# Decoder layer: value projection moved ahead of queries and keys, its place among the first scores taken by context rows

## The chip, the cores and the metric

The kernel runs on one core of one Trainium2 chip. The metric is the device time of one execution in microseconds. Three executions of the kernel before took 847.68, 848.48 and 849.51 us; the median is 848.48 us.

## The reference

One post-norm decoder layer on x (2 sequences of 256 tokens, width 512, fp32) with a context of 2 x 512 rows:

```python
# 1. causal self-attention, 32 heads of 16, ALiBi bias
qkv = x @ w_attn + b_attn                       # w_attn 512 x 1536: q, k, v
scores = einsum('bqhd,bkhd->bhqk', q, k) / 16
attn = softmax(where(causal, scores + slope[h] * (k_pos - q_pos), -inf))
x = layernorm(x + (attn @ v) @ w_proj + b_proj)
# 2. cross-attention: 32 query heads, 8 key/value heads of 128
kv = concat([context, x], axis=1)               # 768 rows per sequence
q = rms_norm(x @ Wq) * q_norm_w;  k = rms_norm(kv @ Wk) * k_norm_w;  v = kv @ Wv
x = layernorm(x + softmax(q k^T / sqrt(128)) @ v @ Wo)
# 3. feed-forward by blocks of a permuted x, 16 blocks of 32 -> 128 -> 32
x = layernorm(x + ffn(x))
```

## The kernel before, in words

All large products are made in three passes of 512 columns on TensorE (`three_passes`, lines 46 to 50): each fp32 operand is split into a high and a low part, and hi x hi, hi x lo and lo x hi are summed in one PSUM bank. So every weight chunk (128 x 512, one of four of a 512 x 512 group) goes through a fixed chain: SP's DMA queue loads it into `w_raw[:, i, :]`, ACT makes `w_hi` (`weights_hi`, line 474), and DVE (`early_lo`, line 617) or POOL (`late_lo`, line 408) makes `w_lo = raw - hi`. There is one raw buffer of four chunks, so the load of chunk i of group p waits until `w_lo` of chunk i of group p - 1 is made (`load_weights`, line 336).

The first stage (the function that the diff touches) computes the self-attention, and at the same time keys and values of the cross-attention for all 12 row tiles of context and x1. Its parts:

- 16 transposes of x (line 802) and their split into `xT_hi` (ACT, line 524) and `xT_lo` (DVE, line 675).
- Q and K, 48 matmuls each: bank 4 + m for the m-th tile of 128 features. ACT takes Q out (`qT`, line 535). K is taken out twice, for even heads by ACT (`kT_even`, line 543) and for odd heads by DVE (`kT_odd`, line 690).
- V, 48 matmuls, by row tile j (`values(j)`, line 821); ACT takes each tile out in two pieces (line 552).
- 16 quads of four heads each. For quad c: scores "S" (line 844, banks 0 to 3, 16 matmuls that stream past 32 rows each); "E" for each of its four heads: DVE adds the bias and takes the maximum (`softmax_shift`, line 628), ACT exponentiates (line 485); "R": DVE makes reciprocals (line 637), POOL multiplies by them (lines 421 and 423) and makes the biases of the next quad (`alibi`, line 416); "T": transposes (line 854), copied out by DVE (line 643); "PV": the product with the values for a pair of quads.
- "part" (n, r): an eighth of the keys and values of context or x1 row tile n, six matmuls. Four column groups (two of Wk, two of Wv) take two parts each. "CT"/"CX" transpose and split a context tile, "KG" copies keys out and squares them on ACT (lines 515 and 520), DVE sums the squares (line 666), POOL normalises (lines 449 and 451), "KT"/"KX" transpose the keys.

The order is written out by one function, `order_of_work`, as a list that every engine walks through, doing only its own share of each entry. Each engine works strictly in that order. S(c + 1) waits until DVE has done all four heads of quad c (`s_out`), since the banks are the same. Bank order beside that is planned in a loop over the list (`RING` banks 4 and 7, `GROUPS` banks 5 and 6).

Weight groups are loaded in the order p = 0, 1, 2 (q, k, v of `w_attn`), 3, 4 (`Wk`), 5, 6 (`Wv`), 7 (`w_proj`), 8, 9 (`Wq`). `ON_VECTOR` lists the groups whose low part is DVE's work; those in `ON_POOL` are POOL's. "W" p in the list is the place where a later group is split. The entry "XT" 1 / "XL" 1 at quads 11 and 12 writes x1's second row tile over the scores' banks; the next scores wait for its low part (DVE, line 721).

Before, the list begins S0, W5, V0, E(0,0), V1, E(0,1), V2, E(0,2), CT0, CX0, V3, E(0,3), R(0,0), W6, R(0,1), and then S1 with part(0,0), E(1,0), T(0,0) and so on.

Of the kernel before, what the change touches and what calls it, by code (L numbers as in the profile page):

```python
# [23 lines left out]
KT = D // P  # L24
# [57 lines left out]
def order_of_work():  # L82

    order = [("S", 0), ("W", 5), ("V", 0), ("E", (0, 0)), ("V", 1), ("E", (0, 1)), ("V", 2), ("E", (0, 2)), ("CT", 0), ("CX", 0), ("V", 3),
             ("E", (0, 3)), ("R", (0, 0)), ("W", 6), ("R", (0, 1))]
# [27 lines left out]

    for c in range(NQ):
# [5 lines left out]
        for i in range(QUAD):  # L120
            late = []
            if mid == 0 and i == 2:
                parts(q % 2)
                copy_keys(q // PARTS, q % PARTS // 2 - 1)
# [6 lines left out]
            elif mid == 1 and i < 3:  # L131
                if i == 1:
                    copy_keys(q // PARTS, q % PARTS // 2 - 1)
# [27 lines left out]
        if c < NQ - 1:  # L161
            parts(1)
# [50 lines left out]
def self_attention_and_keys(nc, d, k):  # L213

    with ExitStack() as ctx:
# [7 lines left out]
        ON_VECTOR, ON_POOL = (0, 1, 2, 4, 6, 8), (3, 5, 7)  # L223
# [60 lines left out]
        before = {4: ("V", 0), 7: ("V", 3), 5: ("V", 1), 6: ("V", 2)}  # L284
# [49 lines left out]
        def _(sp):  # L334
            def load_weights(p):
                name, g = (("w_attn", 0), ("w_attn", 1), ("w_attn", 2), ("Wk", 0), ("Wk", 1), ("Wv", 0), ("Wv", 1),
                           ("w_proj", 0), ("Wq", 0), ("Wq", 1))[p]
                for i in range(KT):
                    if p > 0 and p - 1 in ON_VECTOR:
                        sp.wait_ge(w_los, KT * ON_VECTOR.index(p - 1) + i + 1)  # L340
                    elif p > 0:
                        sp.wait_ge(late_los, KT * ON_POOL.index(p - 1) + i + 1)
# [7 lines left out]
            for i in range(TT):  # L350
                sp.dma_start(x[:, i, :], d["x"].rearrange("b s d -> (b s) d")[tokens(i), :]).then_inc(x_in[i], 16)
# [37 lines left out]
        def _(pool):  # L389
# [38 lines left out]
            late_lo(3)  # L428
            late_lo(5)
# [41 lines left out]
        def _(act):  # L471
# [49 lines left out]

            for j in range(TT):
# [3 lines left out]
            for i in range(KT):  # L526
                weights_hi(0, i)
            act.wait_ge(col_ps, 1)
            nc.scalar.activation(cols[:], bank[:, 7, 0:NCOLS], ACT.Copy).then_inc(col_out, 1)
            for i in range(KT):  # L530
                weights_hi(1, i)
            act.wait_ge(col_out, 1)
# [5 lines left out]
            for i in range(KT):  # L538
                weights_hi(3, i)
            act.wait_ge(nw_made, 2)  # L540
            for m in range(KT):
# [3 lines left out]
                weights_hi(4, m)  # L545
            act.wait_ge(zeros, 2)
            for what, a in ORDER:
                if what == "V":
                    act.wait_ge(v_ps, a + 1)
                    for odds in range(2):  # L550
                        lanes = slice(odds * SA_DIM, (odds + 1) * SA_DIM)
# [1425 lines left out]
```

## Time and profile before

| | before |
|---|---|
| median of three runs | 848.48 us |
| profiled execution, its own time | 847.78 us |
| span of its trace | 846.0 us |
| mean granted TensorE clock | 0.996 |
| PE busy | 825.7 us, 98% of the span |
| DVE, POOL, ACT busy | 547.8, 522.1, 475.4 us |

The span lies 1.8 us below the execution's own time, and the profiled execution is 0.7 us below the median. Times of the trace count from the start of the span. "PE" is the matmul queue, "PEld" its weight loads, "SPq" the issue of DMAs by SP. A timeline row gives start, length, engine, line of the kernel, instruction, output and inputs, and in square brackets the engine's idle time before it with what ended it. The matmuls overlap: a 128x512 matmul is shown with some 0.4 us, but the next begins 0.23 to 0.24 us after it began.

### The profile page before, as it was taken

What the parts mean: (1) busy time and instruction counts of PE and PEld (TensorE: products, weight loads), DVE (VectorE), ACT (ScalarE), POOL (GpSimd) and SP (SyncE); (2) the same over time, 40 slices, a digit from 0 to 9 for tenths busy, and PEclk for the clock granted to TensorE, in tenths of its full rate; (3) what the DMA queues carried; (4) which work ended last, traced back from release to release, by engine and by line L of the source; (5) the groups of instructions that cost most, each with busy time, mean ns of one, the idle gap of its engine ahead of it and who ended that gap; (6) DMA issues with size and microseconds to landing.
All of it is one profiled execution on the core that took longest, in us unless ns stands there. A gap on an engine that the chain in (4) does not pass through costs nothing. (4 is left out here: it accounts for less than half of the span.)

```text
span 846.0 us, 15109 instructions
## 1 busy us (share of the span) xinstructions
PE 825.7 (98%) x4841; PEld 693.0 (82%) x4841; DVE 547.8 (65%) x1505; ACT 475.4 (56%) x1005; POOL 522.1 (62%) x676
## 2 busy tenths in 40 slices
PE   7999999999999999999999999999999999999986
PEld 5777777777788888888888888888888888888764
DVE  4466566765345776667666766677667767777654
ACT  5666665566246565555555555556455645556543
POOL 3577876767336566765766666765775676536741
PEclk9999999999999999999999999999999999999999
DMA  7613223121141721221102101122122102000011
GB/s 226 186 38 117 84 75 109 55 76 51 50 138 54 250 77 38 69 69 39 50 24 86 62 21 68 37 68 68 37 68 68 37 4 76 4 0 1 1 26 50
DMA packets 48510, 56.22 MB, mean 66 GB/s; under 512 B 4670, under 2 KB 29772, under 8 KB 48460
## 3 DMA queue, kind: packets, MB, share of 16 engines
q1 hardware_dynamic: 48460, 55.59, 21.5%
q8 instruction: 27, 0.44, 0.2%
q14 instruction: 23, 0.19, 0.1%
HBM read 41.95 MB, written 13.63 MB: 66 GB/s over the span
## 5 line engine op out<-in xcount | busy, mean ns | idle before, releaser
L1251 POOL TENSOR_SCALAR prob<-prob,x_rinv 128x768 f32<-128x768 f32 x124 | 112.6, 908 | 173.4 <-DVE x_rinv L1425 173.4
L1362 ACT ACTIVATE pT_hi<-bank 128x512 fp32r<-128x512 f32 x192 | 114.3, 598 | 90.1 <-PE bank L1575 90.0
L1345 ACT ACTIVATE prob<-bank,x_nm,q_rms 128x768 f32<-128x768 f32 x124 | 123.3, 995 | 47.2 <-DVE x_nm L1419 46.7
L1465 DVE TENSOR_TENSOR pT_lo<-bank,pT_hi 128x512 fp32r<-128x512 f32 x192 | 130.2, 679 | 5.1 <-ACT pT_hi L1362 3.7
L1416 DVE TENSOR_REDUCE x_mx<-bank 128x1 f32<-128x768 f32 x124 | 118.3, 954 | 22.0 <-PE bank L1529 21.6
L1575 PE MATMUL bank<-ident,prob 128*128 128x128 f32 x768 | 114.8, 272 | 2.1 <-POOL prob L1251 1.3
L1575 PEld LDWEIGHTS bank<-ident,prob 128*128 128x128 f32 x768 | 95.0, 140 | 14.0 <-POOL prob L1251 2.0
L48 PE MATMUL bank<-pT_hi,xv_hi 128*128 128x512 f32 x192 | 86.5, 450 | 1.2 <-DVE pT_lo L1465 0.8
L485 ACT ACTIVATE s_self<-s_self,nm_self 128x128 f32<-128x128 f32 (+1 forms) x128 | 57.1, 448 | 43.1 <-DVE nm_self L628 42.6
L50 PE MATMUL bank<-pT_hi,xv_lo 128*128 128x512 f32 x192 | 75.7, 394 | 0.0
L49 PE MATMUL bank<-pT_lo,xv_hi 128*128 128x512 f32 x192 | 75.4, 393 | 0.0
L1529 PE MATMUL bank<-xk_hi,qT_hi 128*128 128x384 f32 x244 | 65.6, 350 | 0.3 <-ACT prob L1345 0.2
L1529 PE MATMUL bank<-xk_lo,qT_hi 128*128 128x384 f32 x244 | 63.4, 341 | 0.0
L1529 PE MATMUL bank<-xk_hi,qT_lo 128*128 128x384 f32 x244 | 62.7, 337 | 0.0
L48 PE MATMUL bank<-wq_hi,x_hi 128*128 128x512 f32 x144 | 58.8, 408 | 0.0
L1371 ACT ACTIVATE oT_hi<-bank 128x512 fp32r<-128x512 f32 x32 | 19.2, 599 | 69.5 <-PE bank L50 69.5
L50 PE MATMUL bank<-wq_hi,x_lo 128*128 128x512 f32 x144 | 56.6, 393 | 0.0
L49 PE MATMUL bank<-wq_lo,x_hi 128*128 128x512 f32 x144 | 56.4, 392 | 0.0
L48 PE MATMUL bank<-w_hi,cT_hi 128*128 128x512 f32 x128 | 56.0, 437 | 0.0
L643 DVE COPY pT_self<-bank 128x384 f32<-128x384 f32 x64 | 35.4, 554 | 29.3 <-PE bank L854 29.1
L48 PE MATMUL bank<-wo_hi,oT_hi 128*128 128x512 f32 x128 | 52.3, 409 | 0.0
L1529 PEld LDWEIGHTS bank<-xk_hi,qT_hi 128*128 128x128 f32 x244 | 43.5, 189 | 9.5 <-ACT prob L1345 1.5
(227 smaller groups left out, 2043.1 us busy)
## 6 DMA issues: line engine op xcount, KB each, us to landing
wo_raw<-in_Wo SPq DMA_DIRECT2D x8, 1024.0 KB, 5.4
v_by_head<-v_st SPq DMA_DIRECT2D x12, 512.0 KB, 3.3
kT_by_head<-kT_st SPq DMA_DIRECT2D x12, 512.0 KB, 3.2
xk_raw<-kT_by_head SPq DMA_DIRECT2D x16, 384.0 KB, 3.2
xv_raw<-v_by_head SPq DMA_DIRECT2D x16, 384.0 KB, 3.2
wq_raw<-in_Wq SPq DMA_DIRECT2D x6, 1024.0 KB, 5.5
wq_raw<-in_w_attn SPq DMA_DIRECT2D x12, 256.0 KB, 3.9
xk_raw<-in_ctx SPq DMA_DIRECT2D x8, 256.0 KB, 2.6
```

Of the source, the lines that this page charges most:

```text
L48: nc.tensor.matmul(out, a_hi, b_hi, start=first, stop=False)
L49: nc.tensor.matmul(out, a_hi, b_lo, start=False, stop=False)
L50: return nc.tensor.matmul(out, a_lo, b_hi, start=False, stop=last)
L485: nc.scalar.activation(s_sb[:, c % 2, i, a:e], s_sb[:, c % 2, i, a:e], ACT.Exp, bias=nm[:, c % 2, i, qt:qt + 1], scale=-1.0, accum_out=rsu ...
L643: nc.vector.tensor_copy(pT[:, c % 2, i, :], bank[:, bank_of("T", (c, i)), 0:3 * P]).then_inc(pt_out, 1)
L1251: nc.gpsimd.tensor_scalar(prob[:, s, :], prob[:, s, :], rinv[:, s:s + 1], 1.0, ALU.mult, ALU.mult)\
L1345: nc.scalar.activation(prob[:, s, :].rearrange("p (a e) -> p a e", a=2), bank[:, at:at + 2, 0:HALF], ACT.Exp, bias=nm[:, s:s + 1], scale=q ...
L1362: nc.scalar.activation(pT_hi[:, a, :], bank[:, turn.bank[s, what, a], :], ACT.Copy)\
L1416: nc.vector.reduce_max(mx[:, s:s + 1], bank[:, at:at + 2, 0:HALF], AX.XY)\
L1465: nc.vector.tensor_tensor(pT_lo[:, a, :], bank[:, turn.bank[s, what, a], :], f32(pT_hi[:, a, :]), ALU.subtract).then_inc(ring_out, 1)
L1529: last = nc.tensor.matmul(bank[:, at + c, 0:HALF], a_hi[:, g, w], k_part[:, b, c * HALF:(c + 1) * HALF], start=start, stop=stop)
L1575: last = nc.tensor.transpose(bank[:, at, j * P:(j + 1) * P], prob[:, UT * (s % 2) + j, a * P:(a + 1) * P], ident[:])
```

## The change

- The weight groups of `w_attn` are loaded in the order v, q, k. The loads of x and of the v group alternate on SP's queue (x tile 0, chunk 0, x tile 1, chunk 1, ...).
- V is made first, in 16 steps of three matmuls (chunk i, row tile j), as tiles and chunks arrive; the transposes of x tiles 2 and 3 stand among them. ACT and DVE split x tiles and v chunks in turn. Then come the transpose of the bias columns (now into bank 0), Q and K.
- The "V" entries leave the list. CT0 and CX0 go ahead of S0, and two parts stand where two V tiles were. The list begins CT0, CX0, S0, W6, part(0,0), E(0,0), part(0,1), E(0,1), R(0,0), KG(0,0), part(0,2), E(0,2), part(0,3), E(0,3), R(0,1), then S1, KG(0,1), part(0,4).
- Four parts come sooner in that way, and four part entries that stood at the end of quads leave (`if c < NQ - 5`): those ahead of S13, S14, S15, and the one behind T(14,3) in quad 14.
- `w_lo` of groups 3 and 5 moves from POOL to DVE. The split of group 5 moves from the list to the loop that takes K out; groups 3 and 4 are both split between Q's last and K's first eviction.
- The four additions of the projection bias on POOL are no longer behind eight `w_lo`.

Core of the diff:

```diff
-    order = [("S", 0), ("W", 5), ("V", 0), ("E", (0, 0)), ("V", 1), ("E", (0, 1)), ("V", 2), ("E", (0, 2)), ("CT", 0), ("CX", 0), ("V", 3),
-             ("E", (0, 3)), ("R", (0, 0)), ("W", 6), ("R", (0, 1))]
+    order = [("CT", 0), ("CX", 0), ("S", 0), ("W", 6)]
...
+    for i in range(QUAD):
+        parts(1)
+        order.append(("E", (0, i)))
+        if i % 2:
+            order.append(("R", (0, i // 2)))
...
-        if c < NQ - 1:
+        if c < NQ - 5:
             parts(1)
...
-        ON_VECTOR, ON_POOL = (0, 1, 2, 4, 6, 8), (3, 5, 7)
+        ON_VECTOR, ON_POOL = (0, 1, 2, 3, 4, 5, 6, 8), (7,)
...
# SP
-                name, g = (("w_attn", 0), ("w_attn", 1), ("w_attn", 2), ("Wk", 0), ("Wk", 1), ("Wv", 0), ("Wv", 1),
+                name, g = (("w_attn", 2), ("w_attn", 0), ("w_attn", 1), ("Wk", 0), ("Wk", 1), ("Wv", 0), ("Wv", 1),
                            ("w_proj", 0), ("Wq", 0), ("Wq", 1))[p]
                 for i in range(KT):
+                    if p == 0:
+                        sp.dma_start(x[:, i, :], ...)
...
# ACT
             for m in range(KT):
+                weights_hi(2, m)
                 act.wait_ge(qk_ps, m + 1)
                 nc.scalar.activation(qT[:, m, :], bank[:, 4 + m, :], ACT.Identity, bias=cols[:, m:m + 1])\
                     .then_inc(q_out, 1)
-                weights_hi(2, m)
-            for i in range(KT):
-                weights_hi(3, i)
+            for p in (3, 4):
+                for i in range(KT):
+                    weights_hi(p, i)
             act.wait_ge(nw_made, 2)
             for m in range(KT):
                 act.wait_ge(qk_ps, KT + m + 1)
                 nc.scalar.activation(kT_even[:, m, :], ...)
-                weights_hi(4, m)
+                weights_hi(5, m)
...
# PE
+            def values(i, j):
+
+                pe.wait_ge(xt_lo, j + 1)
+                pe.wait_ge(w_los, i + 1)
+                last = three_passes(nc, bank[:, 4 + j, :], xT_hi[:, i, tokens(j)], xT_lo[:, i, tokens(j)],
+                                    w_hi[:, 0, i, :], w_lo[:, 0, i, :], i == 0, i == KT - 1)
...
+            row_transposes(0)
+            row_transposes(1)
+            values(0, 0)
+            row_transposes(2)
+            for i, j in ((0, 1), (1, 0), (1, 1)):
+                values(i, j)
+            row_transposes(3)
+            for i, j in ((0, 2), (1, 2), (2, 0), (2, 1), (2, 2), (0, 3), (1, 3), (2, 3)):
+                values(i, j)
+            for j in range(TT):
+                values(KT - 1, j)
```

DVE before, from the last of K's odd heads to the first shifts of quad 0 (`kT_odd` is K for odd heads, `w_lo` a weight chunk's low part, `s_self` the shifted scores):

```order
L690 TENSOR_SCALAR kT_odd<-bank,cols,odd 128x512
L617 TENSOR_TENSOR w_lo<-wq_raw,w_hi 128x512
L628 ISA s_self,nm_self<-bank,alibi 128x128
L628 ISA nm_self 128x1
L628 ISA s_self,nm_self<-bank,alibi 128x256
```

The same place of the changed kernel (here its line numbers are two or three higher):

```order
L693 TENSOR_SCALAR kT_odd<-bank,cols,odd 128x512
L619 TENSOR_TENSOR w_lo<-wq_raw,w_hi 128x512
L623 TENSOR_TENSOR cT_lo<-bank,cT_hi 128x512
L619 TENSOR_TENSOR w_lo<-wq_raw,w_hi 128x512 x4
L630 ISA s_self,nm_self<-bank,alibi 128x128
L630 ISA nm_self 128x1
L630 ISA s_self,nm_self<-bank,alibi 128x256
```

The low part of context tile 0 and the four low parts of group 6 now stand ahead of the first shift.

PE before, from the transposes T(11,3) (line 854) over part(6,7) to the scores S13 (line 844):

```order
L854 MATMUL bank<-ident,s_self 128x128 x3
L48 MATMUL bank<-w_hi,cT_hi 128x512
L49 MATMUL bank<-w_lo,cT_hi 128x512
L50 MATMUL bank<-w_hi,cT_lo 128x512
L48 MATMUL bank<-w_hi,cT_hi 128x512
L49 MATMUL bank<-w_lo,cT_hi 128x512
L50 MATMUL bank<-w_hi,cT_lo 128x512
L844 MATMUL bank<-kT_odd,qT 128x128 x4
L844 MATMUL bank<-kT_odd,qT 128x256 x4
```

The same place of the changed kernel, from part(7,2) over T(11,3) (now line 870) to S13 (now line 860):

```order
L48 MATMUL bank<-w_hi,cT_hi 128x512
L49 MATMUL bank<-w_lo,cT_hi 128x512
L50 MATMUL bank<-w_hi,cT_lo 128x512
L48 MATMUL bank<-w_hi,cT_hi 128x512
L49 MATMUL bank<-w_lo,cT_hi 128x512
L50 MATMUL bank<-w_hi,cT_lo 128x512
L870 MATMUL bank<-ident,s_self 128x128 x3
L860 MATMUL bank<-kT_odd,qT 128x128 x4
L860 MATMUL bank<-kT_odd,qT 128x256 x4
```

The six matmuls between T(11,3) and S13 have left; part(6,7) now stands in front of T(11,0), at the start of quad 12's scores.

## Rows read from the trace of the kernel before

**Rows 1.** The page: engine totals and the granted clock over 40 slices.
```profile
span 846.0 us, 15109 instructions
...
PE 825.7 (98%) x4841; PEld 693.0 (82%) x4841; DVE 547.8 (65%) x1505; ACT 475.4 (56%) x1005; POOL 522.1 (62%) x676
...
PEclk9999999999999999999999999999999999999999
```

**Rows 2.** Windows: busy time by engine in each stretch, last columns clock and DMA.
```profile
3.36:7.05 3.69, 3.69 (x16) 3.08 (x16) 1.39 (x3) 1.79 (x3) 3.44 (x5) 1.00 1.03 339
7.05:9.15 2.10, 0.00 (x0) 0.03 (x1) 2.10 (x4) 2.06 (x5) 0.45 (x2) 1.00 0.44 165
9.15:10.17 1.02, 1.01 (x4) 0.84 (x5) 1.02 (x3) 0.61 (x2) 0.00 (x0) 0.99 0.23 14
10.17:13.67 3.50, 3.50 (x9) 2.34 (x7) 0.64 (x2) 0.00 (x0) 0.00 (x0) 0.52 0.80 252
13.67:33.70 20.03, 20.03 (x86) 15.88 (x85) 9.62 (x16) 13.17 (x23) 5.08 (x4) 1.00 0.70 213
33.70:57.00 23.30, 22.55 (x131) 17.16 (x134) 12.10 (x48) 16.13 (x50) 16.23 (x21) 1.00 0.26 84
57.00:220.00 163.00, 162.51 (x1192) 126.52 (x1192) 101.90 (x385) 102.11 (x313) 115.40 (x220) 1.00 0.27 81
```

**Rows 3.** Timeline of PE: start, length, instruction, idle before it.
```profile
9.15 0.47 PE L48 MATMUL bank<-x_hi,w_hi 128*128 128x512 f32 x1 [2.10 <-DVE w_lo L617]
...
33.70 0.94 PE L844 MATMUL bank<-kT_even,qT 32*128 32x128 f32 x16
...
46.62 0.94 PE L844 MATMUL bank<-kT_odd,qT 32*128 32x128 f32 x16
...
56.86 0.94 PE L844 MATMUL bank<-kT_even,qT 32*128 32x128 f32 x16 [0.53 <-DVE nm_self L628]
...
176.65 0.94 PE L844 MATMUL bank<-kT_odd,qT 32*128 32x128 f32 x16
```

**Rows 4.** Timeline of ACT, first 40 us.
```profile
4.48 0.60 ACT L524 ACTIVATE x_hi<-bank 128x512 fp32r<-128x512 f32 x1 [2.46 <-PE bank L802]
...
22.57 0.69 ACT L535 ACTIVATE qT<-bank,cols 128x512 f32<-128x512 f32 x1 [1.51 <-PE bank L50]
...
27.53 0.63 ACT L474 ACTIVATE w_hi<-wq_raw 128x512 fp32r<-128x512 f32 x1 [2.05 <-DMA wq_raw<-in_Wk]
28.07 0.76 ACT L543 ACTIVATE kT_even<-bank,even_bias,even 128x512 f32<-128x512 f32 x1
...
33.81 0.78 ACT L543 ACTIVATE kT_even<-bank,even_bias,even 128x512 f32<-128x512 f32 x1 [1.51 <-PE bank L50]
...
39.12 0.63 ACT L474 ACTIVATE w_hi<-wq_raw 128x512 fp32r<-128x512 f32 x1 [2.21 <-DMA wq_raw<-in_Wv]
```

**Rows 5.** Timeline of DVE at 5, 35 and 175 us.
```profile
5.12 0.69 DVE L675 TENSOR_TENSOR x_lo<-bank,x_hi 128x512 fp32r<-128x512 f32 x1 [3.55 <-ACT x_hi L524]
...
35.42 0.68 DVE L617 TENSOR_TENSOR w_lo<-wq_raw,w_hi 128x512 fp32r<-128x512 f32 x1
36.02 0.28 DVE L628 CUSTOM_DVE_ANT_0 s_self<-bank,alibi 128x128 f32<-128x128 f32 x1
...
36.58 0.28 DVE L628 CUSTOM_DVE_ANT_0 s_self<-bank,alibi 128x128 f32<-128x128 f32 x1
...
175.35 0.55 DVE L643 COPY pT_self<-bank 128x384 f32<-128x384 f32 x1
175.82 0.68 DVE L721 TENSOR_TENSOR x_lo<-bank,x_hi 128x512 fp32r<-128x512 f32 x1
```

**Rows 6.** Timeline of the DMA queue of SP: issue of one weight chunk.
```profile
36.13 0.33 SPq L343 DMA_DIRECT2D wq_raw<-in_Wv  x1
```

**Rows 7.** Groups of instructions by line, 13.6 to 60 us: busy, mean ns, idle before.
```profile
L617 DVE TENSOR_TENSOR w_lo<-wq_raw,w_hi 128x512 fp32r<-128x512 f32 x16 | 10.8, 706 | 10.1 <-ACT w_hi L474 10.1
L408 POOL TENSOR_TENSOR w_lo<-wq_raw,w_hi 128x512 fp32r<-128x512 f32 x8 | 10.4, 1326 | 23.1 <-ACT w_hi L474 23.0
L485 ACT ACTIVATE s_self<-s_self,nm_self 128x128 f32<-128x128 f32 (+1 forms) x16 | 7.1, 452 | 2.8 <-DVE nm_self L628 2.8
...
L690 DVE TENSOR_SCALAR kT_odd<-bank,cols,odd 128x512 f32<-128x512 f32 x4 | 3.2, 809 | 6.1 <-ACT kT_even L543 6.1
...
L666 DVE TENSOR_REDUCE k_ss<-k_sq 128x4 f32<-128x512 f32 x2 | 1.4, 686 | 1.3 <-ACT k_sq L520 1.3
...
L520 ACT ACTIVATE k_sq<-k_rows 128x512 f32<-128x512 f32 x2 | 1.3, 634 | 0.1
```

More of the change, by code:

```diff
@@ L131, in order_of_work @@
             elif mid == 1 and i < 3:
-                if i == 1:
+                if i == 1 and q % PARTS in (2, 4):
                     copy_keys(q // PARTS, q % PARTS // 2 - 1)
@@ L283, in self_attention_and_keys @@
         RING, GROUPS = (4, 7), (5, 6)
-        before = {4: ("V", 0), 7: ("V", 3), 5: ("V", 1), 6: ("V", 2)}
+        before = {4: ("K", 0), 7: ("K", 3), 5: ("K", 1), 6: ("K", 2)}
         place, quad, rows_over = {}, 0, {}
@@ L520, in copy_keys, with take_values_of @@
                 nc.scalar.activation(k_sq[:], k_rows[:, w, :], ACT.Square).then_inc(ksq_made, 1)
+            def take_values_of(j):
+                act.wait_ge(v_ps, j + 1)
+                for odds in range(2):
+                    lanes = slice(odds * SA_DIM, (odds + 1) * SA_DIM)
+                    nc.scalar.activation(padded[odds][:, j, :, lanes],
+                                         bank[:, 4 + j, :].rearrange("p (g e) -> p g e", e=2 * SA_DIM)[:, :, lanes],
+                                         ACT.Copy).then_inc(v_out, 1)
             for j in range(TT):
@@ L544, in _ @@
                                      scale=even[:]).then_inc(k_out, 1)
-                weights_hi(4, m)
-            act.wait_ge(zeros, 2)
+                weights_hi(5, m)
             for what, a in ORDER:
[L548 to L551, printed above, removed]
-                        nc.scalar.activation(padded[odds][:, a, :, lanes],
-                                             bank[:, 4 + a, :].rearrange("p (g e) -> p g e", e=2 * SA_DIM)[:, :, lanes],
-                                             ACT.Copy).then_inc(v_out, 1)
-                elif what == "CX":
+                if what == "CX":
                     context_hi(a)
@@ L676, in _ @@
                                         f32(xT_hi[:, :, tokens(j)]), ALU.subtract).then_inc(xt_lo, 1)
-            for p in range(2):
-                for i in range(KT):
-                    early_lo(p, i)
+                early_lo(0, j)
+            for i in range(KT):
+                early_lo(1, i)
             dve.wait_ge(col_out, 1)
@@ L684, in _ @@
             nc.vector.tensor_scalar(even_bias[:], cols[:, KT:2 * KT], even[:], None, ALU.mult).then_inc(nw_made, 1)
-            for i in range(KT):
-                early_lo(2, i)
+            for p in (2, 3, 4):
+                for i in range(KT):
+                    early_lo(p, i)
             for m in range(KT):
@@ L796, in drained, with row_transposes @@
                     pe.wait_ge(vg_late, i[0] + 1)
-            pe.wait_ge(const, 4)
-            for j in range(TT):
+            def row_transposes(j):
                 pe.wait_ge(x_in[j], 16)
@@ L912, in _ @@
             for what, a in ORDER:
-                if what == "V":
-                    values(a)
-                elif what == "S":
+                if what == "S":
                     scores(a)
```

66 lines of the change are left out of this document (29 added, 37 removed).

## The prediction

> **What bounds the kernel now.** I read the page first. PE is busy 825.7 of 846.0 us, 98% of the span, the clock is full in nearly all slices, and the other engines stand between 56 and 65% [rows 1]. So the time is the time of the matmuls plus PE's idle and slow stretches; a change that moves matmuls and adds none can only win or lose there. The windows say where these are: PE sits idle for 2.10 us from 7.05 to 9.15, then runs 3.50 us at a granted clock of 0.52 (the lower of its two levels, 1.2 GHz, but for its edges), is full from 13.67 to 33.70, loses 0.75 us in 33.70 to 57.00 and only 0.5 us in the 163 us behind [rows 2]. The timeline of PE gives the marks that I count from: the first product at 9.15 after 2.10 us of waiting for DVE's low part of the first chunk, scores S0 at 33.70, S1 at 46.62, S2 at 56.86 after 0.53 us of waiting for DVE, S13 at 176.65 [rows 3]. The timelines of ACT, DVE and the DMA queue show the chain of the weights beside it [rows 4 to 6], and the groups by line give durations [rows 7]. All that the change can win lies ahead of 57 us: 2.1 us idle, some 1.6 us of slow clock and 0.75 us of small waits, 4.4 us together.
>
> **Pace of PE.** From 13.67 to 33.70 stand 86 matmuls, of which 84 are whole products, so one takes 0.236 us at full clock [rows 2]. At 0.52 eight matmuls and the small transpose take 3.50 us, 0.427 each: the slow stretch costs 8 x 0.19 = 1.5 us, with the transpose 1.6. V is 48 x 0.236 = 11.3 us, Q and K 22.7 us, a part 6 x 0.236 = 1.42 us.
>
> **Part 1, the head.** The first x tile reaches ACT at 4.48 for 0.60 us [rows 4], DVE at 5.12 [rows 5]. Chunk 0 of v now comes right behind that tile; its high part takes 0.62 us on ACT behind the first activation, its low part 0.7 us on DVE [rows 7], so values(0,0) can begin at about 6.5, in place of 9.15. Of the 16 transposes, 3.69 us at half pace [rows 2], eight are now behind that point: 0.65 us if PE is quick (a T of three takes a quarter of a us), 1.7 if slow. The same 2 MB are loaded first in either order, and what PE waited for at 9.15 was DVE and no load [rows 3]; 12 of the 16 steps of V don't need the last chunk. So I count no wait for data. V ends at 6.5 + 0.65 + 11.3 = 18.5, and K, after 0.2 us for the bias columns, at 41.4. That is the good end. If a slow stretch remains, and PE is half idle before 6.5 as it was in 7.05 to 9.15, the end is 1.7 later, 43.1. The trace doesn't say which; what ran before the drop was idle 2.1 us, what will run here is idle 1 to 2 us between tiles. I take the middle, 42.25, and keep both.
>
> **Part 2, the first quad.** Call the end of K T. Before, the last K tile left PE at 33.7, and behind S0 stood V with 11.3 us, under which the softmax of quad 0 and the last weights went unseen. Now only four parts stand there, 5.7 us, and more is queued ahead of the softmax. I follow the chain, each step by a row:
> - Groups 3 and 4 are both split before `kT_even` of tile 0. The low part of the last k chunk is made 0.7 us before Q's end (it follows ACT's third `qT`). From the issue of a load to the activation that waited for it are 36.13 to 39.12, 2.99 us [rows 4, 6]. So group 3's last high part starts 2.35 us after Q's end; its low part is ready at 3.95; group 4's last high part starts at 7.0, `kT_even` 0.54 us later, as in 27.53 to 28.07 [rows 4], at 7.5. Then ACT alternates `kT_even` 0.76 us and group 5's high parts 0.62 us, and waits for group 5's first two chunks too. It ends the last `kT_even` at T + 1.9, where it was T + 0.9 before (33.81 + 0.78 against 33.70 [rows 4]).
> - ACT then makes the last high part of group 5, until T + 2.5, and the context's; DVE `kT_odd` 0.81, the low part 0.7, the context's low part 0.69 [rows 7]: part(0,0) can begin at T + 4.3. PE has only CT0 and S0 until T + 1.6. **Idle 2.7 us.**
> - The last chunk of group 6 is issued when group 5's low part is done, T + 3.7. It lands 2.99 us later, its low part is done at T + 8.0, and only now may DVE start quad 0: five instructions behind it in the queue, as the order shows.
> - Two heads' shifts take 0.56 us each (36.02 to 36.58 [rows 5]), two heads' exponentials 1.0 each (two of 452 ns and the reading of the sums [rows 7]), then the reciprocal, the third head, then KG and its square 0.6 us each on ACT and the sum 0.69 on DVE [rows 7], which now stands ahead of the fourth head. That is 5.4 us: **S1 at T + 13.35.** PE is through with its four parts at T + 4.3 + 5.7 = T + 10.0. **Idle 3.4 us.**
>
> Against before: S1 then stood at 46.62 with four parts (5.66 us) less behind it. So at this mark the changed kernel is 42.25 + 13.35 - 5.66 - 46.62 = 3.3 us late (2.5 by the quick head, 4.2 by the slow one).
>
> The Trainium skill (DMA: Bandwidth & Descriptors, in its account of the two cost components) puts a transfer at about 2.0 us plus bytes over 436 GB/s. For the 256 KB chunk this gives 2.6 us as an estimate; the trace has 2.99 from issue to use. By the page S1 would be some 0.4 to 0.8 us sooner, since two or three landings stand in the chain. The measured number stands in my sum.
>
> **Part 3, small waits that go.** The 0.75 us that PE lost in 33.70 to 57.00 [rows 2], of which 0.53 ahead of S2 [rows 3], should vanish, since nine parts now stand before S2 in place of five. -0.7.
>
> **Part 4, quads 12 to 15.** The four parts used early are missing late. At S13 this costs: before, DVE copied T(11,3) from 175.35, made x1's low part until 176.50 [rows 5], and S13, which waits for it, came at 176.65 [rows 3]; six matmuls stood between. Without these PE is ready at 175.25 and waits 1.25 us. S14, S15 and the T behind them lose 1.42 us of cover each. How much of it they needed no row says; below it is 0, above 0.53 each for the three places, the one wait for DVE's shifts that the trace has [rows 3]. They have no x1 tile in their way and PE lost little from 57 to 220 [rows 2], so I take 0.1. Together +1.35; at best +0.2, if DVE runs ahead by its lighter load; at worst +3.
>
> **Part 5, POOL and DVE.** Eight low parts leave POOL (1.33 us each) and cost DVE 0.7 each [rows 7]. Both are hidden under Q and K except for what is counted above. If POOL's time for the bias additions had been needed, it would show at T(0,0): no.
>
> **Part 6, the clock after the idle time.** Idle 2.10 us was followed by half clock once [rows 2]; here come 2.7 and 3.4 us, with 5.7 us of matmuls between. A slow stretch under the parts costs nothing, since S1 waits for DVE anyway; one behind S1 costs 1.6. Between 0 and 1.6 I take 0.8. The Trainium skill (TensorE: Matmul & The Clock Gate, Part 1) has the throttled state as the default, from which activity releases; the page speaks against this change, and by it the dear end, 1.6, would be the one to take.
>
> **Sum.** +3.3 - 0.7 + 1.35 + 0.8 = +4.8 us. On the profiled execution of 847.8 (its span of 846.0 and 1.8 us around it) this is 852.6; the median of the runs lies 0.7 above that execution, so the forecast is 853.3, rounded to 853.2. Its own range is 850.5 to 856.
>
> **Rivals.**
> - *More stalls than I count.* All at their dear ends: 4.2 - 0.7 + 3 + 1.6 = +8.1, so 856.5. For it: DVE and ACT lose their cover at five places, and S2 waited 0.53 us although five parts stood around S1 [rows 3], where the last quads now have four. Against: in 57 to 220 us PE lost only 0.5 us [rows 2]. 0.17.
> - *The weights come sooner.* If landings take nearer 2 us, ACT has no backlog and S1 comes 2.3 us sooner, at T + 11; with shorter idle time the clock's 0.8 goes too. +1.7: 849.5, or 850.2 with the 0.7 of the median. For it: the loads of groups 4 and 6 run almost alone. Against: the 2.99 us is of such a lone load. 0.19, half of it on either side of the bound below.
> - *Faster: the stall in quad 0 stays hidden.* One mechanism: PE reaches S1 almost without a pause. S1 at T + 10.2 is the point from which it decides, since 41.4 + 10.2 - 5.66 - 46.62 - 0.7 + 1.35 = 0. At T + 7.5, the bare work of CT0, S0 and four parts, the kernel gains 2.7 us: 845.5. For it: the head gives 2.65 us for certain and may save the slow stretch. Against: DVE's queue holds group 6 ahead of the first shift, and that group's load can't be issued before T + 2.4 even without a backlog. 0.14.
> - *The change only reorders full work.* The head's gain and the stalls cancel, 848.5. This is the near end of the case of sooner weights, and counted there.
>
> **How the numbers follow.** Forecast 0.50, more stalls 0.17, weights sooner 0.19, faster 0.14. A measurement of this kernel tells 0.2%, 1.7 us, from no change: the bounds are 846.8 and 850.2. Slower by more: 0.50 + 0.17 + half of 0.19 = 0.77; within: the other half, 0.09; faster: 0.14. The range takes in the middle of the dear case and most of the cancelled one, 846.5 to 858.
>
> **What would show it.** The first matmul of 512 columns at 6.5 us; K's end at 41.4 to 43.1; idle time of PE before part(0,0), ended by DVE's low part of the context, of 2 to 3 us; idle before S1, ended by DVE's shifts, of 3 to 4 us, and before it ACT waiting for `Wv`'s last chunk; S13 waiting 1.2 us for DVE. I am wrong if S1 follows its parts within 0.5 us, if K ends after 44, or if quads 2 to 11 wait by more than 1 us in all.

## The result

The changed kernel took 858.21, 858.60, 859.79 and 859.87 us, a median of 859.19; the kernel before, run beside it on the same chip, 848.46. The ratio is 1.0125, interval 1.0112 to 1.0138: 10.7 us slower, where the forecast was 4.8 us slower. It lies above the range of the forecast, 846.5 to 858 us.

The profiled execution took 859.79 us, 1.8 us more than its span. The page of the changed kernel, to be held against [rows 1]:

```profile
span 858.0 us, 15124 instructions
...
PE 827.9 (96%) x4841; PEld 695.1 (81%) x4841; DVE 555.6 (65%) x1513; ACT 476.3 (56%) x1005; POOL 513.4 (60%) x668
...
PEclk9989999999999999999999999999999999999999
```

PE has the same 4841 matmuls and 2.2 us more of busy time, over a span 12.0 us longer. So most of the loss is idle time. The windows (columns as in [rows 2]) say where:

```profile
6.50:11.08 4.58, 4.58 (x15) 3.89 (x16) 2.19 (x5) 2.24 (x4) 1.25 (x3) 1.00 0.67 207
...
44.50:48.92 4.42, 0.96 (x17) 0.57 (x17) 4.17 (x7) 4.18 (x8) 0.00 (x0) 0.97 0.58 183
48.92:52.00 3.08, 3.08 (x7) 2.45 (x8) 1.75 (x3) 0.82 (x2) 0.00 (x0) 0.50 0.56 179
52.00:58.40 6.40, 4.11 (x18) 3.01 (x16) 4.01 (x20) 4.30 (x15) 2.23 (x6) 1.00 0.02 5
58.40:62.30 3.90, 3.90 (x22) 2.61 (x23) 0.82 (x5) 2.97 (x10) 3.82 (x7) 0.56 0.00 0
...
75.00:220.00 145.00, 139.73 (x1061) 108.23 (x1060) 91.66 (x354) 89.28 (x281) 100.92 (x193) 1.00 0.27 79
```

Four facts stand here. Ahead of S1, 44.50 to 58.40, PE is idle for 3.46 and 2.29 us. After each of the two idle times the granted clock drops to about half (0.50 and 0.56 of these windows, the 1.2 GHz level but for their edges). And behind 75 us, where [rows 2] had lost 0.5 us in 163, 5.27 us are lost in 145. The fourth is at the head. The column of the granted clock says 1.00 for 6.50 to 11.08, but the products there begin 0.43 us apart, as they do at a granted clock of 0.50 (49.48, 49.91), and 0.23 us apart behind it. The same holds for the x transposes of before (3.36 to 7.05, [rows 2]). Why the column differs there no run shows; I call such a stretch half pace. The timeline of PE, against [rows 3], names each:

```profile
3.44 1.09 PE L805 MATMUL bank<-ident,x_rows 128*128 128x128 f32 x4 [3.44 <-DMA x_rows<-in_x]
6.44 1.12 PE L805 MATMUL bank<-ident,x_rows 128*128 128x128 f32 x4 [1.92 <-DMA x_rows<-in_x]
7.21 0.78 PE L48 MATMUL bank<-w_hi,x_hi 128*128 128x512 f32 x1
7.79 0.63 PE L49 MATMUL bank<-w_lo,x_hi 128*128 128x512 f32 x1
8.21 0.63 PE L50 MATMUL bank<-w_hi,x_lo 128*128 128x512 f32 x1
...
11.15 0.39 PE L49 MATMUL bank<-w_lo,x_hi 128*128 128x512 f32 x1
11.38 0.39 PE L50 MATMUL bank<-w_hi,x_lo 128*128 128x512 f32 x1
...
44.52 0.94 PE L860 MATMUL bank<-kT_even,qT 32*128 32x128 f32 x16
48.92 0.77 PE L48 MATMUL bank<-w_hi,cT_hi 128*128 128x512 f32 x1 [3.46 <-DVE cT_lo L623]
58.40 0.85 PE L860 MATMUL bank<-kT_odd,qT 32*128 32x128 f32 x12 [2.29 <-DVE nm_self L630]
...
69.74 0.39 PE L860 MATMUL bank<-kT_even,qT 32*128 32x128 f32 x4
...
157.03 0.50 PE L48 MATMUL bank<-w_hi,cT_hi 128*128 128x512 f32 x1 [1.25 <-DVE v_st L659]
165.94 0.50 PE L48 MATMUL bank<-w_hi,cT_hi 128*128 128x512 f32 x1 [1.05 <-ACT v_st L510]
183.02 0.39 PE L860 MATMUL bank<-kT_even,qT 32*128 32x128 f32 x4 [1.21 <-DVE x_lo L724]
193.24 0.39 PE L860 MATMUL bank<-kT_odd,qT 32*128 32x128 f32 x3 [1.34 <-DVE x_lo L724]
```

The last four rows and two waits of 0.2 us (at 106 and 203 us) make up the 5.27 us. From S15 at 211.69 on, the two kernels run alike, but for one part that the changed kernel has already made by then (1.42 us). ACT, its share of the chain ([rows 4] before):

```profile
41.03 0.76 ACT L557 ACTIVATE kT_even<-bank,even_bias,even 128x512 f32<-128x512 f32 x1
...
51.82 0.63 ACT L477 ACTIVATE w_hi<-wq_raw 128x512 fp32r<-128x512 f32 x1 [1.30 <-DMA wq_raw<-in_Wv]
...
53.82 0.41 ACT L488 ACTIVATE s_self<-s_self,nm_self 128x128 f32<-128x128 f32 x1 [1.37 <-DVE nm_self L630]
...
165.31 0.57 ACT L510 ACTIVATE v_st<-bank 128x512 f32<-128x512 f32 x1
```

DVE ([rows 5] before):

```profile
48.09 0.69 DVE L623 TENSOR_TENSOR cT_lo<-bank,cT_hi 128x512 fp32r<-128x512 f32 x1
...
52.48 0.69 DVE L619 TENSOR_TENSOR w_lo<-wq_raw,w_hi 128x512 fp32r<-128x512 f32 x1 [1.24 <-ACT w_hi L477]
53.09 0.28 DVE L630 CUSTOM_DVE_ANT_0 s_self<-bank,alibi 128x128 f32<-128x128 f32 x1
...
155.81 0.56 DVE L645 COPY pT_self<-bank 128x384 f32<-128x384 f32 x1 [0.52 <-PE bank L870]
156.29 0.68 DVE L659 COPY v_st<-bank 128x512 f32<-128x512 f32 x1
...
182.19 0.68 DVE L724 TENSOR_TENSOR x_lo<-bank,x_hi 128x512 fp32r<-128x512 f32 x1
```

The issue of the last chunk of `Wv` and, right behind it, of the next context tile, on SP's queue ([rows 6] before):

```profile
48.20 0.33 SPq L350 DMA_DIRECT2D wq_raw<-in_Wv  x1
48.57 0.43 SPq L355 DMA_DIRECT2D xk_raw<-in_ctx  x1
```

The bill, from the marks. S1 stands 58.40 - 5.66 - 46.62 = 6.1 us late (5.66 us of parts stand behind it that were in front). S1 to S2 takes 11.34 us, where before it took 56.86 - 46.62 = 10.24 and where an execution of the same order without half clock takes 9.78 (below). So the half clock behind S1 costs 1.6, and 0.5 of small waits of before is gone. Behind S2 the parts (5,6) and (6,0) wait 1.25 and 1.05, S12 waits 1.21, S13 1.34, two others 0.4 together: 5.3, of which the 0.5 that before lost there goes off. 6.1 + 1.6 - 0.5 + 5.3 - 0.5 = 12.0, the difference of the spans.

### The profile page after: what moved, and what is told of

Read it like the earlier page. It is cut to its first block and busy times, and to the rows that moved or that the text cites. A ratio compares the mean times of both kernels' runs of the same rounds, so it can differ in the third digit from the quotient of the medians.

```text
span 858.0 us, 15124 instructions
## 1 busy us (share of the span) xinstructions
PE 827.9 (96%) x4841; PEld 695.1 (81%) x4841; DVE 555.6 (65%) x1513; ACT 476.3 (56%) x1005; POOL 513.4 (60%) x668
## 5 line engine op out<-in xcount | busy, mean ns | idle before, releaser
L426 POOL TENSOR_SCALAR s_self<-s_self,rinv_self 128x128 f32<-128x128 f32 x64 | 24.0, 375 | 50.2 <-DVE rinv_self L639 49.5
```

## Experiments

All ratios are to the kernel before, timed on the same chip in the same job. The intervals are some 1.3 us to either side, so a difference of about 2 us between two experiments is only just told; marks of the trace are those of single executions, and differ by up to 0.9 us between kernels that are alike up to them (K's end stood at 43.50 to 44.43 us in seven of them). The changed kernel's own ratio is 1.0125.

**Group 6 behind quad 0's softmax.** Theory: its last chunk holds DVE's first shifts.

```diff
-    order = [("CT", 0), ("CX", 0), ("S", 0), ("W", 6)]
+    order = [("CT", 0), ("CX", 0), ("S", 0)]
...
             order.append(("R", (0, i // 2)))
+    order.append(("W", 6))
```

> The changed kernel with one edit: the split of weight group 6 (W6) stands behind quad 0's softmax instead of ahead of it. Theory A (W6's last chunk, which lands at 51.82 us, holds DVE's first shift at 53.09 and with it S1 at 58.40): the first shift starts right behind the context's low part at about 48.8, S1 comes 4 us sooner, near 54.3, and the slow clock behind S1 goes (1.6 us) or moves: 853.5 to 855.5 us. Rival B (quad 0's chain is long in itself, and W6 only fills a hole in it): S1 stays within 1 us of 58.4, the time within 1 us of 859.2. If W6 in its new place is late for part(0,6), a new wait of 1 to 3 us stands there and 855.5 to 857 is to be seen.

Measured: 856.81 us, 1.0094 [1.0079, 1.0110]. PE's rows of it:

```profile
56.43 0.39 PE L861 MATMUL bank<-kT_odd,qT 32*128 32x128 f32 x4 [0.15 <-DVE nm_self L631]
...
61.98 0.30 PE L871 MATMUL bank<-ident,s_self 128*128 128x128 f32 x1 [0.88 <-DVE pT_self L646]
```

S1 follows its parts with 0.15 us of waiting, so group 6 was what held it longest. But S1 comes only 2.0 us sooner, where theory A had 4: the parts ahead of it still begin at 48.98 (3.31 us idle) and ran at half clock until 52.49, ACT waited 2.25 us for them before it could copy the first keys (at 53.59), and the sum of these keys' squares stands ahead of the fourth head on DVE. 0.9 us comes back as a wait of T(0,2) for DVE, which now has group 6 in its queue there. The half clock behind S1 did not come.

**The four part entries taken out elsewhere.** Theory: quads 9 to 13 wait because they lost their parts.

```diff
-        if c < NQ - 5:
+        if c < NQ - 1 and c not in (1, 2, 5, 7):
```

> The changed kernel, but the four parts used in quad 0 are taken from behind quads 1, 2, 5 and 7 in place of quads 11 to 14, so that from quad 8 on every engine has the list of the kernel before. Theory A (the waits at 157, 166, 183, 193 and 203 us, 5.1 us in all, come from the order that the shifted parts make there): all five go, none above 0.5 us comes at quads 2 to 8, 854 to 855 us. Rival B (they are later echoes of the first quad's delay, or of DVE's eight added low parts): they stay, 858 to 860. Rival C (any quad with four parts stalls by about 1.3 us): they go and four like them come at S3, S4, S7 and S9, 858 to 860.

Measured: 859.14 us, 1.0115 [1.0100, 1.0131], not told apart from the changed kernel. All four late waits are gone, and new ones stand elsewhere, the two longest ahead of T(2,0) and T(4,0):

```profile
84.95 0.30 PE L870 MATMUL bank<-ident,s_self 128*128 128x128 f32 x1 [2.62 <-DVE x_lo L651]
...
109.79 0.33 PE L870 MATMUL bank<-ident,s_self 128*128 128x128 f32 x1 [1.25 <-POOL s_self L428]
```

With three more of 0.27 to 0.72 us they make 5.4 us behind 75 us, where the changed kernel lost 5.27. That is rival C in its sum, though not at its places. Four parts used early are missing somewhere; in these two placements where they go decides who waits, and not how much.

**Values of context tile 5 copied out a few entries sooner**, on both engines. Theory: the waits at 157 and 166 us are not lack of work. Part (5,6) needs the bank of part (5,4), which is emptied by the `v_st` copy at 156.29, and that stands behind the copy of the T's bank at 155.81 in DVE's queue; part (6,0) needs ACT's `v_st` copy at 165.31 in the same way. "VG" is DVE's copy, "VL" ACT's; the last four lines take them out of their old places.

```diff
+                order.append(("VG", 5))
                 order.append(("Y", (0, 0)))
...
+                if i == 2:
+                    order.append(("VL", 5))
                 order.append(("Y", (1, i - 1)))
...
-                if r == 0 and n >= 1:
+                if r == 0 and n >= 1 and n != 6:
...
-                if r == 6:
+                if r == 6 and n != 5:
```

> The changed kernel with the two evictions of row tile 5's values moved a few entries ahead: DVE's in front of Y(0,0), ACT's in front of Y(1,1). Theory A (at 157.03 and 165.94 part(5,6) and part(6,0) wait for banks whose eviction stands behind the transposes' copies and the exponentials in the engines' order, because Y breaks the alternation of the two banks): both waits go, -2.3 us, 856.5 to 857.5. Rival B (DVE and ACT are simply full there): the waits of 1.25 and 1.05 us move to T or S of quads 9 and 10, 858.5 to 859.5.

Measured: 854.60 us, 1.0064 [1.0049, 1.0080]. Both waits are gone, a new one at 169.88 is 0.63, and S12 waits 0.72 (1.21). The spans differ by 4.4 us: 2.5 behind S2, which are the waits, and 1.9 ahead of it, of which the clock is 1.6. The expectation of the time (856.5 to 857.5) counted the waits alone and was missed by that much. Here S1 waited nearly as long as in the changed kernel, and no half clock followed:

```profile
58.08 0.39 PE L871 MATMUL bank<-kT_odd,qT 32*128 32x128 f32 x3 [2.05 <-DVE nm_self L639]
...
67.86 0.39 PE L871 MATMUL bank<-kT_even,qT 32*128 32x128 f32 x3
```

S1 to S2 is 9.78 us, where the changed kernel took 11.34. This gives the price of one such stretch, 1.56 us. Nothing was edited ahead of S2. The other profiled executions whose order behind S1 is that of the changed kernel fall on the same two values: 9.76 to 9.78 in the sixth, seventh and eighth experiment, 11.38 and 11.31 in the second and the fifth.

The same execution says something of the head. x tile 1 was there early, and the first product waited for DVE's low part instead:

```profile
4.97 1.12 PE L816 MATMUL bank<-ident,x_rows 128*128 128x128 f32 x4
6.95 0.77 PE L48 MATMUL bank<-w_hi,x_hi 128*128 128x512 f32 x1 [0.86 <-DVE w_lo L628]
```

K ended at 44.43 all the same, 0.4 later than in the changed kernel. In the second experiment tile 1 was used at 5.11, and K ended at 43.93.

**Groups 5 and 6 by halves, spread over the softmax of quad 0** (group 4 as before, in the loop that takes K out).

```diff
-    order = [("CT", 0), ("CX", 0), ("S", 0), ("W", 6)]
+    order = [("CT", 0), ("CX", 0), ("S", 0)]
...
             order.append(("R", (0, i // 2)))
+            order.append(("W", 5 + i // 2))
...
-            for p in (3, 4): ... weights_hi(p, i)
+            for i in range(KT): weights_hi(3, i)
...
-                weights_hi(5, m)
+                weights_hi(4, m)
```

> The changed kernel with the weight groups split where they were split relative to the work before: group 4 in the loop that takes K out, group 5 behind E(0,1), group 6 behind E(0,3), all low parts still on DVE. Theory A (ACT and DVE enter quad 0 late by their backlog of groups 4 and 5, and then wait for group 6): kT_even of tile 0 starts right at that tile's end, part(0,0) waits 1 to 1.5 us in place of 3.46, S1 comes at 52 to 53.5, no slow clock behind it: 851.5 to 853.5 us. Rival B (the eight low parts that moved from POOL to DVE are the cost): no more than 1 us is won against the run with W6 alone moved. Rival C (the landing of the later groups becomes the bound: part(0,4) or part(0,6) waits for it): 854 to 856.

Measured: 856.14 us, 1.0083 [1.0069, 1.0097]. ACT's backlog ahead of K is gone: part(0,0) begins 3.2 us after K's end, with 1.78 us idle. S1 is at 55.11, 3.3 us sooner, and still waits 1.92 us, because four low parts now stand ahead of the third head's shift on DVE (rows below). Half clock follows it (S1 to S2 11.36 us), which takes back the 1.3 us that S1 comes sooner than with group 6 alone moved. So theory A (851.5 to 853.5) was missed, and the time is only 0.7 us below the first experiment, as rival B had it. That the low parts moved to DVE are the cost, as B says, is not so: the last experiment moves them back and loses 4 us.

```profile
50.40 2.70 DVE L619 TENSOR_TENSOR w_lo<-wq_raw,w_hi 128x512 fp32r<-128x512 f32 x4 [0.34 <-ACT w_hi L478]
53.03 0.27 DVE L630 CUSTOM_DVE_ANT_0 s_self<-bank,alibi 128x128 f32<-128x128 f32 x1
```

**x ahead of the weights.** Theory of the late first product: the loads of x tile 1 and chunk 0 compete.

```diff
+            for i in range(TT):
+                sp.dma_start(x[:, i, :], ...)
             load_weights(0)          # without the loads of x between
```

> The changed kernel with the loads in the order of before: four x tiles, then the four chunks of v. Theory A (alternating the loads makes x tile 1 land late, at 6.44 us, and brings a chunk that PE can't use before that tile): the transposes of tile 1 begin near 5.3, values(0,0) waits for chunk 0 until about 8, K ends at 43.5 to 44.5 as before: 858.5 to 859.5 us. Rival B (the alternation is what gives the head its gain): K ends 1 us or more later, 860.2 or above.

Measured: 860.15 us, 1.0134 [1.0118, 1.0149]. The first product waits 2.77 us for `w_lo` and begins at 8.39 in place of 7.21. K ends at 44.87 (43.99). Alternating the loads is worth 1.2 us at the first mark and 0.9 at the second, though the time is not told apart from the changed kernel's; it is no cause of the loss.

**Identity transposes in the head's gaps** (4 ahead of x tile 0, 8 behind it, into a free bank), so that PE has work while it waits.

```diff
+            fill(7, 4)
             row_transposes(0)
+            fill(7, 8)
             row_transposes(1)
```

> The changed kernel with 12 transposes of the identity that nothing reads, 4 on PE ahead of x tile 0 and 8 between tiles 0 and 1, into a bank that is free then. Theory A (V starts at half clock, 7.21 to 11.08 us, because PE was idle ahead of it): the clock is full from about 7 to 8 us, K ends 1.3 to 2 us sooner, 857 to 858 us. Rival B (data and not the clock sets V's head: DVE's low parts of tiles 2 and 3): K ends within 0.5 us of 43.99, 858.7 to 859.5.

Measured: 857.31 us, 1.0098 [1.0081, 1.0116]. The products run at full pace from 8.8 us and no longer from 11.1, and K ends at 42.68 in place of 43.99, inside the bracket of the forecast. Of these 1.3 us, 1.0 is pace (from the first product to K's end 35.77 in place of 36.78) and 0.3 an earlier first product, 6.91. The profiled execution, 855.70, also had no half clock behind S1, which waited only 0.45. Of the five executions the fastest took 854.88 and the slowest 858.41 us.

**The same at part(0,0) and S1** (20 and 16 transposes).

```diff
                 if what == "S":
+                    if a == 1:
+                        pe.wait_ge(kg_out, 1)
+                        fill(5, 16)
                     scores(a)
+                    if a == 0:
+                        pe.wait_ge(k_out, 3)
+                        pe.wait_ge(k_odd_out, 3)
+                        fill(6, 20)
```

> The changed kernel with 36 transposes of the identity that nothing reads, 20 between S0 and part(0,0), 16 between part(0,3) and S1, where PE is idle. Theory A (the two slow stretches at 48.63 to 52.04 and 58.87 to 62.28 follow from that idle time, and only the second costs time): neither is seen, S1 stays at 58.4 (+-0.5), S2 comes 1.6 us sooner, 857 to 858.2 us. Rival B (the slow stretches come for another reason): they stay, and the fill adds up to 0.5 us: 859 to 860.

Measured: 856.92 us, 1.0096 [1.0081, 1.0112]. After 10.34 us there is no half clock at all, and theory A holds:

```profile
45.37 2.38 PE L930 MATMUL bank<-ident 128*128 128x128 f32 x20 [0.40 <-DVE kT_odd L693]
47.88 0.47 PE L48 MATMUL bank<-w_hi,cT_hi 128*128 128x512 f32 x1
...
55.24 1.97 PE L930 MATMUL bank<-ident 128*128 128x128 f32 x16 [1.63 <-ACT k_rows L518]
57.42 0.39 PE L860 MATMUL bank<-kT_odd,qT 32*128 32x128 f32 x4 [0.22 <-DVE nm_self L630]
```

S1 to S2 is 9.78 us. S1 itself is 1.0 us sooner; 0.5 of that is an earlier K's end in this execution.

**x1's low part ahead of the last transposes of quads 11 and 12.**

```diff
-            order.append(("T", (c, i)))
             if mid in (2, 3) and i == 3:
                 order.append(("XL", mid - 2))
+            order.append(("T", (c, i)))
```

> The changed kernel with DVE's low part of x1 tiles 0 and 1 ahead of its copy of T(10,3) and T(11,3), not behind it. Theory A (S12 and S13 wait 1.21 and 1.34 us for that low part, which stands behind the copy of 0.55 us and the wait for the transposes): the waits fall to about 0.5 to 0.7 each, 857.8 to 858.5 us. Rival B (S12 and S13 would wait for DVE's shifts next anyway): the waits stay near 1.2 with another releaser, within 0.3 us of 859.2.

Measured: 856.82 us, 1.0099 [1.0082, 1.0116]. S12 waits 0.73 in place of 1.21, S13 0.24 in place of 1.34: 1.6 us less. The profiled execution (855.19) had 1.97 us of idle time ahead of S1 and no half clock behind it. The four executions are 855.19, 855.74, 857.90 and 858.19, at mean clocks of 0.997, 0.997, 0.995 and 0.995. That would fit a half clock behind S1 in the two slow ones, but it is not shown: they have no trace, and the mean clock does not say where it fell. In the third experiment the fastest execution (853.32) had 0.994 and the slowest (855.37), which is the profiled one, 0.997.

**The kernel before with 18 transposes** between its own x transposes and Q. Its 2.10 us of idle time is filled.

```diff
+            for _ in range(18):
+                nc.tensor.transpose(bank[:, 7, 0:P], ident[:], ident[:])
             pe.wait_ge(xt_lo, TT)
```

> The kernel before with one addition: 18 transposes of the identity that nothing reads, on PE between the last x tile and the first product, where it idles from 7.05 to 9.15 us. Theory A (the half clock from 10.17 to 13.67 follows from that idle time and costs 1.6 us): no slow stretch there, first product still at 9.1 to 9.3, S0 at 32.1 in place of 33.7: 1 to 1.6 us faster than before, ratio 0.998 to 0.999. Rival B (the stretch comes from the state that PE starts in): it stays, ratio 1.000 to 1.0005.

Measured over 11 executions: 847.08 us, 0.9986 [0.9977, 0.9995], faster than both kernels. First PE's timeline, then the windows:

```profile
7.01 2.67 PE L805 MATMUL bank<-ident 128*128 128x128 f32 x18
9.44 0.48 PE L48 MATMUL bank<-x_hi,w_hi 128*128 128x512 f32 x1
```

```profile
7.00:9.44 2.44, 2.44 (x20) 2.44 (x19) 2.24 (x4) 2.18 (x6) 0.51 (x2) 1.00 0.57 214
9.44:32.46 23.02, 23.02 (x101) 18.04 (x99) 11.83 (x19) 14.03 (x24) 5.06 (x4) 1.00 0.72 220
```

The clock stays full, and the products begin 0.23 us apart, where before the granted clock was 0.52 for 3.50 us [rows 2]. The x transposes ahead of the gap ran at half pace as before (3.65 us), so rival B is out. The first product is 0.29 us later (9.15 before), S0 1.24 us sooner (32.46 against 33.70), the span 1.3 us shorter. These 18 transposes gained more than moving V did even with its mends (next experiment).

**All four mends together** (values sooner, x1's low part first, head filled, weights spread).

> The changed kernel with four of the edits together: values' evictions sooner, x1's low part ahead of the copy, fill on PE at the head, and the weight groups split where they were (5 behind E(0,1), 6 behind E(0,3)). Theory A (the losses stand at separate places and add): -2.8 (quads 9 and 10), -1.6 (S12, S13), -1.3 (head), -3.3 (first quad), and up to 1.6 of slow clock: 848.5 to 850.5 us on a chip where the changed kernel takes 859.2, a ratio of 1.000 to 1.002 to before. Rival B (PE gets ahead and the next wait takes the place of the one mended): ratio 1.004 or more, with waits elsewhere.

Measured over 11 executions: 850.46 us, 1.0023 [1.0014, 1.0032]. K ends at 42.19, S1 stands at 53.06 (5.3 us sooner than in the changed kernel), the waits behind 75 us are 1.6 us in place of 5.3. At S2 the kernel is 5.3 us ahead, and 4.1 more are won behind it: 9.4 us, the difference of the spans (848.6 against 858.0). The mends add up, but the kernel is still 1.8 us slower than before. PE still waits 1.77 us ahead of part(0,0) and 1.91 ahead of S1, and half clock follows S1 (11.37 us to S2).

**The same with group 5 split chunk by chunk between the heads**, to take the four low parts away from one place.

```diff
-            order.append(("W", 5 + i // 2))
+        order.append(("W1", (5, i)))
+    order.append(("W", 6))
```

> As the run with all mended, but group 5 is split one chunk behind each of quad 0's four heads instead of all four behind E(0,1). Theory A (in the run with the groups spread, S1 came at T + 10.9 and not T + 8.6 because four chunks on ACT and DVE stood ahead of the third head): S1 comes 0.8 to 1.5 us sooner than in the run with all mended, the time 0.5 to 1.5 us lower, ratio 0.999 to 1.001. Rival B (the work is the same and S1 waits for the fourth head either way): within 0.4 us of that run.

Measured: 855.91 us, 1.0087 [1.0073, 1.0100], 5.4 us worse than by halves, which neither expectation had. S1 stands 13.5 us behind K's end, where by halves it stood 10.9 behind. ACT and DVE now wait for each other in turn, as in this row of ACT:

```profile
50.80 0.41 ACT L493 ACTIVATE s_self<-s_self,nm_self 128x128 f32<-128x128 f32 x1 [1.37 <-DVE nm_self L642]
```

A part behind S1 waits 1.49 us for a low part of the late group 6, and S1 to S2 is 2.8 us longer than by halves. The profiled execution is 2.0 us above the median of its five: there x tile 1 landed at 7.10 and K ended at 44.17, where with the same head it had landed by 5.88 and K had ended at 42.19. In the sixth experiment, with the same head too, it was used at 6.20 and K ended at 42.68. So with the gaps filled K's end goes with that tile. Without the fill it does not: K ended at 43.50 to 44.43 in seven executions in which tile 1 was used at 4.97 to 6.46.

**Low parts of groups 3 and 5 back on POOL**, in the changed kernel.

```diff
-        ON_VECTOR, ON_POOL = (0, 1, 2, 3, 4, 5, 6, 8), (7,)
+        ON_VECTOR, ON_POOL = (0, 1, 2, 4, 6, 8), (3, 5, 7)
```

> The changed kernel with the low parts of groups 3 and 5 back on POOL, behind the first biases. Theory A (the move to DVE is a gain of its own: POOL takes 1.33 us where DVE takes 0.7, and the next group's loads wait for it): group 6's last chunk lands 1 to 3 us later, S1 comes later by as much or more, 860.5 to 863 us. Rival B (the eight low parts on DVE are what makes the change slow): S1 comes sooner, 856 to 858.5.

Measured: 863.53 us, 1.0175 [1.0159, 1.0191]. So this part of the change wins about 4 us by itself. On POOL the additions of the bias come late again, beside DVE's low parts. First DVE, then POOL:

```profile
49.62 0.77 DVE L621 TENSOR_TENSOR w_lo<-wq_raw,w_hi 128x512 fp32r<-128x512 f32 x1
50.93 2.85 DVE L621 TENSOR_TENSOR w_lo<-wq_raw,w_hi 128x512 fp32r<-128x512 f32 x2 [0.54 <-ACT w_hi L479]
54.22 1.27 DVE L621 TENSOR_TENSOR w_lo<-wq_raw,w_hi 128x512 fp32r<-128x512 f32 x1 [0.44 <-ACT w_hi L479]
```

```profile
49.79 6.85 POOL L438 TENSOR_TENSOR x_rows<-x_rows,pT_self 128x512 f32<-128x512 f32 x4
```

Three of DVE's four low parts take 1.27 to 1.43 us each while POOL runs its additions, and 0.69 in the same place of the changed kernel, where POOL had made them by 24.65. S1 is at 61.14, 2.7 us later than in the changed kernel, with 4.37 us idle ahead of it. 1.4 of that is there already at CT0 (45.36 for 43.99), which waits 0.95 us for `kT_odd`.

## Why the forecast was wrong in size

The direction was right, and so was the chain through the first quad. Four terms of the sum were too small, and in the largest the mechanism was missing for most of the loss.

- **Part 1, the head: "I take the middle, 42.25".** The sum was 1.7 us short: K ended at 43.99. The half pace came in full and not by half, from the first product to 11.08, and the first product came at 7.21 for 6.5. From it to K's end were 36.78 us, where the quick head of the sum has 34.9; filling the gaps gave 35.77. I had taken the middle although all that had run before the drop in [rows 2] was idle time, and more of it was coming. "So I count no wait for data" was wrong too (x tile 1 was waited for until 6.44, 1.92 us of idle time), but it was not what made K late: with that tile at 4.97 and 5.11 the first product still came at 6.95 and 6.82, behind DVE's low part, and K at 44.43 and 43.93.
- **Part 2, the first quad: mechanism right, size 1.1 short.** Each link was there in its order: `kT_even` at 41.03, idle time ahead of part(0,0) ended by the context's low part, ACT waiting for `Wv`'s last chunk, its low part ahead of the first shift, S1 waiting for `nm_self`. From the first shift to S1 were 5.31 us (5.35 in the sum). What was off is the load: issued 4.2 us after K's end (3.7), and 3.62 us from issue to use (48.20 to 51.82) where I used 2.99. The load of 2.99 was issued while the DMA engines were idle (busy share 0.00 from 36 to 37 us); this one stood between others (the context tile at 48.57 on SP's queue, a share of 0.59 to 0.80 from 48.00 to 50.50). That their company made it slower is not shown. The Trainium skill (DMA: Bandwidth & Descriptors, the two cost components, a fit of loads issued from GpSimd) gives an estimate of 2.6 us for 256 KB; both loads measured, issued from SP, are slower, and the measurement decides. (Two or three landings at 0.39 us less each would be 0.8 to 1.2 us by that estimate; the forecast wrote 0.4 to 0.8, outside its sum.) PE's wait at S1 was 2.29 and not 3.4 although S1 was late itself, because its parts began 0.6 us later and took 1.4 us longer at half clock.
- **Part 3, small waits: right in kind.** S2 follows without a wait. S1 to S2 without half clock is 0.5 us shorter than before, and not 0.7: the rest lay ahead of S1 and was in the first term already.
- **Part 4, the late quads: "I take 0.1" for all but S13. The step that failed most, 3.4 us** (1.35 in the sum; 5.3 measured, less the 0.5 that before lost there, is 4.8). S13 was right (1.34 for 1.25). S12 I had not looked at: x1's first tile has the same entry one quad sooner, and it waits 1.21. And "PE lost little from 57 to 220" was used as evidence that nothing stood close to waiting there. That row shows what PE waited for, not how near the others were. The two `v_st` waits, 2.3 us, come neither from missing cover for S nor from DVE's load, but from two engines' strict order: where the projection's rows ("Y" in the list) took one of the two banks in turn, the next column group of the parts needed the bank of the group just before it, with the values still in it. The forecast named its sign (quads 2 to 11 waiting by more than 1 us) and gave it no price. The third experiment shows it: both waits go. The second shows that S12 and S13 wait for lack of the four parts; the eighth, that 1.6 of their 2.55 us can be won back by the order on DVE.
- **Part 5, POOL to DVE: hidden, as said**, but more than that. It is a gain of 4 us against the same kernel with those low parts on POOL (last experiment). Seen there are DVE's own low parts at up to double their length beside POOL's additions, and group 5 late. The forecast counted neither.
- **Part 6, the clock: 0.8 taken, 1.6 came** in the profiled execution. The Trainium skill (TensorE: Matmul & The Clock Gate, Part 1) has the throttled state as the default, which the forecast read as the dear end, and the changed kernel's trace agrees with that (0.56 in 58.40 to 62.30 behind 2.29 us of idle time). The traces of the third and the eighth experiment don't, with 2.05 and 1.97 us of idle time at the same place and full clock behind it, while 1.97 in the fifth and 1.91 in the tenth were followed by half clock. So a chance, and not a certainty, was the right form. The same section of that page says that how much of a kernel runs slow varies from run to run; these traces, of kernels that are alike there, agree.

The excess is 1.7 + 1.1 + 0.2 + 3.4 + 0.8 = 7.2 on top of 4.8, the 12.0 of the bill. The medians differ by less, 10.7, because the profiled execution is 0.6 us above its median and before's 0.7 below its own. The rival "more stalls than I count" was the nearest, and still 2.7 us short: it let each known place reach its dear end and had none for a place not listed.

What stays open: what decides whether half clock follows the idle time ahead of S1; why the granted clock reads 1.00 over the half pace of the first 11 us; why x tile 1 was used at 4.97 to 7.10 us in different executions of the same load order; and how much of the last experiment's loss is the bias additions beside DVE and how much group 5's slower low parts, since both were moved at once.

## What to carry to other kernels

Where each engine walks through one list, work that is moved forward must be paid back where it stood, and what it hid there is found only by asking of every entry behind it how close it was to waiting: a PE that waits for nothing shows no margins. Count what is queued ahead of the moved work's consumers on every engine, and whether a bank is still free one entry sooner. If TensorE must wait early in the program, a few transposes of the identity into a free bank can be worth more than reordering the products (0.9986 here, against 1.0125, and 1.0023 with all mends).

## What the runs showed of the hardware

- 1.91 to 2.29 us of idle time on TensorE ahead of S1 was followed by 3.4 us at a granted clock of 0.50, or, behind 1.97 and 2.05 us, by none, in executions of kernels that are alike there. One stretch cost 1.56 us here. Transposes in the gaps brought full pace to the head of the changed kernel 2.3 us sooner (8.8 for 11.1). In the seventh and the ninth experiment no half clock followed a gap that held them; in the eleventh, where 0.91 us of idle time came behind eight of them, the first products still ran at half pace, from 7.87 to 10.8.
- A 256 KB load took 3.62 us from issue to use with others around it, where one issued while the DMA engines were idle took 2.99 [rows 4, 6].
- DVE's subtraction of a 128x512 chunk took 0.69 us alone and 1.27 to 1.43 us, in three cases of four, while POOL added tiles of the same size, whose additions took 1.71 us each on average for 1.26 before. The Trainium skill (GPSIMD Engine Reference, Specifications) names such contention for DVE instructions with two inputs in SBUF, as this one has; the rows agree, and give its size.
